# Deformable-convolution kernel: bilinear weights turned by DMA transposes, next images' preparation placed by a table over three images

## What is computed

```python
# layer 0: channel attention on the group-normalized image
q, k, v = split(gn(x) tokens @ w_qkv.T)           # each (192, 1024) per image
attn = softmax(einsum('bcn,bdn->bcd', q, k) * SCALE)
x = x + (w_out @ (attn @ v) + b_out)
# layer 1: modulated deformable 3x3 convolution on the group-normalized result
offset = clip(conv3x3(gn(x), off_w) + off_b, -8, 8)     # 18 channels: y and x of 9 taps
mask = 2 * sigmoid(conv3x3(gn(x), mask_w) + mask_b)     # 9 channels
y = sum over 9 taps of w[tap] @ bilinear_sample(gn(x), pixel + tap + offset) * mask, + proj_b
# batch norm over all 32 images, then exact GELU
x = x + gelu(batchnorm(y) * gamma + beta)
```

## Time and profile before

| | us |
|---|---|
| three runs, median (lowest to highest) | 4007.24 (3994.69 to 4007.55) |
| profiled execution, its own time | 3993.97 |
| its span | 3992.2 |

### The profile page before, as it was taken

The page is one execution under the profiler, slowest core; times in us unless marked ns, Lnnn a source line. Parts: engine busy times, 40 slices in busy tenths (PEclk is TensorE's granted clock), DMA queues, the critical chain, the costliest instruction groups (busy, mean ns, idle before and its releaser), DMA issues.

```text
span 3992.2 us, 110012 instructions
## 1 busy us (share of the span) xinstructions
PE 3544.1 (89%) x38338; PEld 3034.8 (76%) x38338; DVE 2646.4 (66%) x5834; ACT 2111.3 (53%) x4790; POOL 1412.8 (35%) x1165
## 2 busy tenths in 40 slices
PE   3999999999999999999999999999999999999700
PEld 2788887888888888888888888888888888888700
DVE  3577766676677667677766676677667667766522
ACT  1555555565555555555555565555555555555432
POOL 1333333343433333333333343333333333333311
PEclk8999999999999999999999999999999999999955
DMA  2000000000000010000000000000000001000299
GB/s 63 20 10 28 28 27 22 28 28 19 20 28 28 20 28 28 28 10 28 28 20 28 28 28 15 23 28 28 20 28 28 28 10 28 28 20 18 76 377 322
DMA packets 50722, 170.05 MB, mean 43 GB/s; under 512 B 9664, under 2 KB 10880, under 8 KB 50176
## 3 DMA queue, kind: packets, MB, share of 16 engines
q1 hardware_dynamic: 39584, 136.75, 11.2%
q0 software_dynamic: 7168, 25.17, 1.6%
q10 hardware_dynamic: 3424, 0.90, 0.1%
HBM read 87.29 MB, written 75.50 MB: 41 GB/s over the span
## 4 chain that ended last, share of the span: by engine, by line
PE 66%; DVE 12%; issue 9%; DMA 4%; POOL 3%; ACT 3%; DVEq 1%; SPq 1%; ACTq 0%; POOLq 0%
PE sps L666 10%; PE acc L683 6%; PE acc L685 6%; PE acc L684 6%; PE l L594 4%; PE zps L652 3%; PE zps L656 3%; PE zps L653 3%; PE zps L655 3%; PE zps L654 3%; DVE zl L1155 3%; DMA xn<-x_scratch 2%; POOL sT L1343 2%; DVE sl L1161 2%; PE l L526 2%
## 5 line engine op out<-in xcount | busy, mean ns | idle before, releaser
L1343 POOL TENSOR_TENSOR sT<-ay,bx 128x768 f32<-128x768 f32 x768 | 1149.5, 1507 | 1363.4 <-PE sps L666 1292.5
L1161 DVE TENSOR_TENSOR sl<-sps,sh 128x384 f16<-128x384 f32 x1536 | 846.0, 551 | 563.8 <-ACT sh L905 557.7
L683 PE MATMUL acc<-zh,sh 128*128 128x192 f16 x4608 | 1133.7, 246 | 0.9 <-issue 0.6
L685 PE MATMUL acc<-zh,sl 128*128 128x192 f16 x4608 | 1133.6, 246 | 0.0
L684 PE MATMUL acc<-zl,sh 128*128 128x192 f16 x4608 | 1133.6, 246 | 0.0
L905 ACT CAST sh<-sps 128x384 f16<-128x384 f32 x1536 | 741.7, 483 | 695.3 <-PE sps L666 689.6
L871 ACT CAST zh<-zps 128x288 f16<-128x288 f32 x1536 | 620.4, 404 | 638.8 <-PE zps L656 611.7
L1155 DVE TENSOR_TENSOR zl<-zps,zh 128x288 f16<-128x288 f32 x1536 | 693.2, 451 | 334.3 <-ACT zh L871 325.4
L666 PE MATMUL sps<-eye,sT 128*128 128x128 f32 x4608 | 785.8, 279 | 127.2 <-DVE sl L1161 99.4
L666 PEld LDWEIGHTS sps<-eye,sT 128*128 128x128 f32 x4608 | 530.9, 140 | 283.5 <-DVE sl L1161 167.9
L684 PEld LDWEIGHTS acc<-zl,sh 128*128 128x128 f16 x4608 | 450.9, 98 | 17.7 <-issue 0.8
(11 more groups left out here) (200 smaller groups left out, 6482.7 us busy)
## 6 DMA issues: line engine op xcount, KB each, us to landing
xin<-in_x SPq DMA_DIRECT2D x32, 512.0 KB, 5.4
xin<-in_x SPq DMA_DIRECT2D x64, 256.0 KB, 6.0
x_scratch<-x SPq DMA_DIRECT2D x32, 512.0 KB, 2.7
y_scratch<-ych SPq DMA_DIRECT2D x32, 512.0 KB, 2.7
zh<-y_scratch SPq DMA_DIRECT2D x20, 512.0 KB, 11.1
zl<-x_scratch SPq DMA_DIRECT2D x20, 512.0 KB, 12.5
out<-zh POOLq DMA_DIRECT2D x20, 512.0 KB, 8.6
x_scratch<-x SPq DMA_DIRECT2D x32, 256.0 KB, 3.4
```

The costliest lines, as they stand in the source:

```text
L683: pe.matmul(acc[:, 0:C], s_h, zh[:, j, ky, z], start=start and kx == 0, stop=False)
L685: mm = pe.matmul(acc[:, 0:C], s_l, zh[:, j, ky, z], start=False, stop=stop and kx == 2)
L1161: dve.tensor_tensor(one(sl), sps[u % 2][:, 0:3 * P], one(sh), ALU.subtract).then_inc(s_lo, 1)
L1343: pool.tensor_tensor(sT[:, p % ST_RING].rearrange("p k (r x) -> p k r x", r=R), a, x_, ALU.mult)\
```

## The change

1. **S is turned by DMA.** POOL writes float32 S to `s32`; ScalarE makes the high part and VectorE the low part straight from SBUF, next to each other in `spm` (128 x 2 x 768, float16), and one DMA transpose on SyncE's queue per step (`turn_s`, L499) turns the twelve 128 x 128 blocks into `sT`. TensorE's transposes and the banks `sps` are gone. A step is two units (`STEPS` = 24 an image). Rings: 2 of `s32`, 3 of `spm`, 4 of `sT`; a step's transpose is issued three steps ahead, and waits for the matmuls of the step four before it.
2. **Z in whole steps.** The two freed banks go to `zps`, so that one copy and one subtraction take 576 columns in place of 288; five steps ahead in place of ten halves.
3. **Places by table.** `part0` takes its units from `PE_AT`, `ACT_AT`, `DVE_AT`, `POOL_AT`, `SP_AT`, from -17 to 71, and `prepare` runs it for three images at once: the end of this one's preparation, the next one's, the start of the one after. The residues are cut in two halves (L1096); the second half of the hats is made during the image that uses them.
4. **Smaller moves.** Scaling y (`scale_y`) goes from VectorE to ScalarE; the stores and loads on SyncE are placed between the transposes; `rmat` shares `t1`'s memory; the far path uses other scratch.

```diff
+STEPS = 3 * TILES
+LEAD, TAIL = 17, 24
+PE_AT = {
+    "group": (-10, 21), "turn_x": (3, 3, 4, 5), "gram": 7, "t1": 9, "logits": 9, "r": 12, "m": 13,
+    "apply": (15, 16, 17, 18), "offsets": (35, 35, 35, 36, 36, 37, 37, 37), "offset_max": 11,
+}
...
+DVE_AT = {
+    "loaded": (-17, -16, -16, -14), "moments": (-12, 20), "variance": (-10, 20),
+    "residue": ((-4, -3, -1, -1), (24, 24, 26, 28)), "gram": 6, "max": 9, "softmax": 10, "m": 13,
...
-        ST_RING = 3
-        sT = sb("sT", [P, ST_RING, 3, R * W])
-        S_RING = 3
-        sh = sb("sh", [P, S_RING, 3, P], F16)
-        sl = sb("sl", [P, S_RING, 3, P], F16)
+        S_RING, H_RING = 2, 3
+        s32 = sb("s32", [P, S_RING, 3 * R * W])
+        spm = sb("spm", [P, H_RING, 2, 3 * R * W], F16)
+        T_RING = 4
+        sT = sb("sT", [P, T_RING, 12, P], F16)
...
+        def prepare(part0, u, b, par, more):
+
+            if u < TAIL:
+                part0(u + UNITS, b, par)
+            if more:
+                part0(u, b + 1, 1 - par)
+            if more == 2 and u >= UNITS - LEAD:
+                part0(u - UNITS, b + 2, par)
...
+            def turn_s(p, b):
+                sp.wait_ge(s_lo, STEPS * b + p + 1)
+                sp.sem_inc(lo_seen, 1)
+                if p >= T_RING or not first(b):
+                    sp.wait_ge(sz_done, STEPS * b + p - T_RING + 1)
+                    sp.sem_inc(slot_free, 1)
+                sp.dma_start_transpose(sT[:, p % T_RING], spm[:, p % H_RING].rearrange("p i n -> p (i n)"))\
+                  .then_inc(turned(b, p)[0], 16)
...
-            def turn_s(u, b):
-                t, ky, c = u // 6, u % 6 // 2, u % 2
+            def convolve(p, c, b, par):
+                i, ky = p // 3, p % 3
                 if c == 0:
-                    pe.wait_ge(st_made, 24 * b + 3 * t + ky + 1)
-                if u >= 2 or not first(b):
-                    pe.wait_ge(s_lo, UNITS * b + u - 1)
-                g = (3 * t + ky) % ST_RING
-                for kx in range(3):
-                    mm = pe.transpose(sps[u % 2][:, kx * P:(kx + 1) * P], sT[:, g, kx, c * P:(c + 1) * P], eye32[:, :])
-                mm.then_inc(s_ps, 1)
...
+                    pe.wait_ge(*turned(b, p))
...
+            def split_s(p, b):
+                act.wait_ge(st_made, STEPS * b + p + 1)
+                if p >= H_RING or not first(b):
+                    act.wait_ge(*turned(b, p - H_RING))
+                act.copy(spm[:, p % H_RING, 0], s32[:, p % S_RING]).then_inc(s_hi, 1)
...
+            def split_s(p, b):
+                dve.wait_ge(s_hi, STEPS * b + p + 1)
+                dve.tensor_tensor(spm[:, p % H_RING, 1], s32[:, p % S_RING], spm[:, p % H_RING, 0], ALU.subtract)\
+                   .then_inc(s_lo, 1)
...
+            def make_s(p, b, par):
...
+                if p >= S_RING or not first(b):
+                    pool.wait_ge(s_lo, STEPS * b + p - S_RING + 1)
```

More of the change, by code:

```diff
@@ L184, in build @@
         yt = bank("yt")
-        zps = bank("zps", (P, 2, 512))
-        sps = [bank(f"sps{i}") for i in range(2)]
+        zps = bank("zps", (P, 4, 512))
         l0 = [bank(f"l0_{i}") for i in range(2)]
@@ L1093, in part0 @@
-                if u == 27:
+                for q in range(4):
+                    if u == at["x1"][q]:
+                        m, n = q // 2, slice(q % 2 * 512, q % 2 * 512 + 512)
+                        dve.wait_ge(mx_ps, 4 * b + q + 1)
+                        if q == 0 and not first(b):
+                            dve.wait_ge(x1_stored, 32 * b)
+                        dve.scalar_tensor_tensor(out=x1[:, m, n], in0=l0[(q + 1) % 2][:, :], scalar=bo[:, m:m + 1],
+                                                 in1=xin[:, m, n], op0=ALU.add, op1=ALU.add).then_inc(x1_sb, 1)
@@ L1111, in part0 @@
+                for k in range(3):
+                    if u == at["move"][k]:
+                        if k == 0 and not first(b):
+                            dve.wait_ge(off_ps, b)
+                        dve.wait_ge(xn_lo, 4 * b + 2 + k)
+                        moved = move(k, b, par)
+                        if k == 2:
+                            moved.then_inc(x2_moved, 1)
+                if u == at["offsets"]:
                     dve.wait_ge(off_ps, b + 1)
@@ L1257, in part1 @@
                         flag = is_far(dve, b, par)
[L1258 to L1266 removed]
+                    for q in range(4):
+                        if u == DVE_AT["y_stats"][q]:
+                            if q < 2:
+                                y_stats(q, b, par)
+                            elif not first(b):
+                                y_stats(q, b - 1, 1 - par)
+                    prepare(part0, u, b, par, more)
                 where_far(flag, dve, b, par, more, far_pass, (fz_lo, FAR_Z), (f_st, 3 * TILES), (fs_lo, FAR_UNITS),
@@ new lines, in part1 @@
+            def part1(b, par, more):
+                lead = S_AHEAD + 1
+                if first(b):
+                    for p in range(lead):
+                        make_s(p, b, par)
+                for p in range(STEPS):
+                    if p + lead < STEPS:
+                        make_s(p + lead, b, par)
+                    elif more:
+                        make_s(p + lead - STEPS, b + 1, 1 - par)
+                    for u in (2 * p, 2 * p + 1):
+                        prepare(part0, u, b, par, more)
```

544 lines of the change are left out of this document (278 added, 266 removed).

## The result

| | median us | lowest to highest | ratio to before |
|---|---|---|---|
| before | 4002.57 | 3994.69 to 4007.55, 4 runs | |
| after | 3865.98 | 3857.68 to 3880.1, 4 runs | 0.9664 [0.963, 0.9699] |

The change saves 137 us of 4003. The forecast was 3438 us, in a range of 3290 to 3790: the direction came out, the size did not, and the time lies outside the range.

A forecast was written before the change was run, and what follows sets the result against it. TensorE, busy 89% of the span, bounds the kernel: period 115.5 - 15.8 (transposes) - 2.0 (stalls) = 97.7 us; head 97.3, 31 periods and last part 299.1 give 3425.1, as a median 3438 us, range 3290 to 3790.

The forecast's parts named there:

- Three transposes leave each of 48 units: On TensorE, removing the transposes of S saves 0.33 us a unit, 15.8 us an image.
- The prices of the pieces: Costs of the larger instructions on VectorE and ScalarE, giving 70.7 and 62.4 us an image, both under TensorE's 97.7.
- rival (a): VectorE and POOL get in each other's way: subtractions of S wait up to 1332 ns; 3625 us, chance 0.17.
- 1.8 and, for issue, up to 3 us: On SyncE's queue, the cost of one step's DMA transpose, against 4.07 us available a step.
- (b): The queue of transposes sets the pace at 4.07 to 4.8 us a step; 3760 us, chance 0.12.
- (c): Transposes go one at a time, 5.4 us each, and TensorE's clock could fall; 4430 us, chance 0.10.
- (d): Transposes cut into small pieces or blocks one by one, 14.6 us a step; 11,260 us, chance 0.02.
- the stall term: TensorE's idle time before L666, 4.0 us an image: between all and none comes back, half taken, 2.0 us.
- lands some 5 us late, within the 12.2: On SyncE, the transpose behind layer 0's stores and x loads is late but covered by the three-step lead; no cost.
- SyncE's waits: Waits for x1 and y hold up queued transposes, but are placed after VectorE's step, so costed at nothing.
- (e): The table wins back all 4.0 us of stalls and 3.5 us of other waits; 3267 us, chance 0.05.
- (f): Spreading the work does nothing for the stalls: period 99.7 us, 3501 us; shares chance 0.54 with the forecast.

The follow-up runs named there:

- e7_half: The changed kernel with a second transpose a step, of the six low blocks into a spare tile, ahead of each real one; 4048.16 us, ratio 1.0117.
- e12_third: The kernel before with one of three TensorE transposes of S a unit kept from the second image on; 3809.76 us, ratio 0.9519.
- e1_spread: The changed kernel with SyncE's plain DMAs placed one to a unit between the transposes; 3796.6 us, ratio 0.9487.
- e2_moments: The changed kernel with VectorE's moments one unit earlier, ahead of its wait for the offset convolution; 3746.17 us, ratio 0.9338.
- e11_idle: The changed kernel with plain DMAs spread, moments earlier, residues spread, offset-dependent work moved later and ScalarE's share moved into its idle time; 3657.01 us, ratio 0.9152.
- e6_bunched: The changed kernel with the next image's work bunched as in the kernel before, three units earlier; 4095.15 us, ratio 1.0226.
- e4_oneblock: The changed kernel with only one of a step's twelve blocks transposed, the others left zeros; 3759.52 us, ratio 0.94.

## Why the prediction was wrong

**Right.** "Three transposes leave each of 48 units: 48 x 0.33 = 15.8 us": 15.7 for the transposes themselves, 14.5 for all of TensorE's own work. The prices of the pieces: VectorE's subtraction of S 958 ns, measured 1006; Z's 750, measured 753; ScalarE's copy of S 0.93, measured 0.833, and of Z 0.64, measured 0.639. POOL 1567 ns for 1507. With them rival (a) falls: the two alternate as supposed (1474.0 of POOL's 1615.3 us of idle time before L1418 end with a subtraction), and a subtraction costs 48 ns more than was worked out and not 1332. The step's transpose "1.8 and, for issue, up to 3 us": the queue's share rose to 58.1% of 16 x 3878.3 us from 11.2% of 16 x 3992.2, that is 36,053 - 7,154 = 28,899 us of engine time, by 768 and 16 engines 2.35 us, a third over the 1.8; 1.42 us to issue; landing in

```profile
sT<-spm SPq DMA_TRANSPOSE x768, 3.7
```

us, under the 5 of the forecast. Rivals (b), (c) and (d) fall by this and by e7_half. DMA share went to 0.59, a little over the "fifth to a half".

On the two readings of the Trainium skill that the forecast set side by side: twelve blocks in one DMA do not take twelve times the 1309 ns of the Trainium skill ("VectorE: DVE Perf Modes", The three transpose paths), they land in 3.7 us. The 261 GB/s of the Trainium skill ("DMA: Bandwidth & Descriptors", Latency and other measured facts) would have given 1.5 us of transfer; here 393 KB took 2.35 us of the engines, 167 GB/s. Neither changed the outcome.

**Wrong, first: the stall term.** "The bounds are 4.0 us back and none ... I take half, 2.0." The bound was on the wrong side of the sign. The stalls grew from 7.5 to 14.3 us an image. The forecast read stalls before one line, L666, and took their sum as all there was to win or lose; the other engines' waits for TensorE (1292.5 us of POOL's, 689.6 of ScalarE's before S alone) were taken as slack. They are slack only while TensorE stays slow: e12_third speeds up TensorE alone, and 6.0 us come of 10.5. Applied to the changed kernel's 15.7 us, 35 to 43% would be an estimated 5 to 7 us an image that no term carried.

**Wrong, second: "lands some 5 us late, within the 12.2", by which SyncE's five DMAs were costed at nothing.** The lateness was about right: 2.4 us in the queue and 2.8 more in flight, 5.2. The 12.2 us were not there to take it. The chain in them (POOL 1.5, ScalarE 0.8, VectorE 1.0, landing 3.7) takes 7.0 even if no piece waits; the text had named these pieces but had not subtracted them before it said "within". And the pieces do wait in their queues: at unit 30 the low part was ready 5.6 us before its use, 5.6 - 3.7 = 1.9 us were left, and 5.2 - 1.9 = 3.3 of the measured 3.5 us follow. The five issues keep the queue from 1526.06 to 1531.20 us. e1_spread prices it at 69 us.

**Wrong, third: what stands in a queue behind a wait.** The forecast costed SyncE's waits one by one, but not VectorE's. The wait for the offset convolution at unit 36 with the moments behind it is worth 120 us (e2_moments), and it could be read from the table and from the order of VectorE's instructions, with TensorE's places beside them. After it, ScalarE's load from unit 41 to the image's end is likely next (e11_idle).

**Left out: the clock.** It stood only in rival (c). It is read in four windows of the changed kernel, behind the stalls of units 30 and 39:

```profile
1537.00:1541.00 4.00, 3.19 (x21) 2.87 (x22) 3.03 (x4) 0.83 (x1) 2.54 (x2) 0.65 1.11 210
1541.00:1545.00 4.00, 4.00 (x39) 3.41 (x37) 2.62 (x9) 1.37 (x2) 0.20 (x1) 0.92 0.52 97
1560.00:1564.00 4.00, 3.90 (x19) 3.64 (x20) 2.43 (x7) 1.84 (x5) 0.86 (x3) 0.50 0.18 35
1564.00:1568.00 4.00, 4.00 (x35) 3.32 (x33) 1.37 (x6) 2.04 (x4) 0.27 (x2) 0.81 0.37 67
```

After the idle 3.4 us at unit 39 TensorE works at 0.50, the 1.2 GHz level, through the next 4 us, though it is busy in 3.90 of them. The rest column rose by 3.8 us an image. How much of it is clock and how much small waits the runs do not part.

**The account.** Span forecast 3425.1, measured 3878.3, missing 453.2 us: 31 x (111.3 - 97.7) = 422, the last part 30, the head 1. Of the 13.6 us a period, 8.8 are the stalls (6.8 more, not 2.0 fewer), 3.8 the rest, and 1.3 TensorE's own work, not the transposes but the small products; these three come from images 4 to 27 and add to 13.9. By the prediction's own test, "TensorE's main wait is not for its own queue" and "the period is over 105", it had failed. "The table does better than half" had a rival for it (e) and "the spreading does nothing" another (f), but none for the case that came: spreading is worth 229 us against the bunched order of e6_bunched and still does not bring the stalls back to what they were.

## What to carry to other kernels

When the full engine gets faster, take its saving as an upper end and look for what runs a unit late behind it: here 6.0 of 10.5 us came through with nothing else changed. For each instruction that waits on the fast engine, list what stands behind it in its queue and who needs that soon; one place in a table was worth 3% of the time. Against a lead, first subtract the chain as it stands in the queues (here 5.6 us of 12.2 were left behind VectorE's part, and 3.7 of them are flight), and only then the lateness; and put a long series of plain DMAs nowhere in a row ahead of one that is waited for.

## What the runs showed that was not expected

- The clock: TensorE runs at 0.50 for some 4 us behind a stall of 3.4 us and at 0.81 for the next 4, which costs some 2.8 us again (an estimate, 4 x 0.50 + 4 x 0.19, as if all of TensorE's work there went by the clock). In the kernel before, whose longest wait within the image loop is 1.17 us, the clock stays at 1.00.
- VectorE's small SBUF instructions are lengthened too: the 128x2 products at 1557.80 and 1558.68 took 0.81 and 1.36 us, where the medians of both lines are 0.16. POOL ran two instructions over them, and each of the two products ended within 0.02 us of one of these (at 1558.59 and 1560.03). Of three copies of the same shape in the units in which the image is moved, one takes four times as long as the others, in every image but the first; it starts 0.17 us after a product of POOL (1539.61 to 1541.20 us) and ends 0.3 us behind it. The subtraction of S, which alternates with POOL, is hardly touched:

```profile
L1106 DVE COPY x2s_lo_a<-x_lo_a 128x992 f16<-128x992 f16 x32 | 53.7, 1678 | 0.0
L1106 DVE COPY x2s_hilo_b<-x_hilo_b 128x992 f16<-128x992 f16 x32 | 14.1, 440 | 0.0
```

- DMA transposes scale with their blocks: twelve cost 2.35 us of the sixteen engines. In e7_half the extra six blocks a step took (78.6% x 4042.5 - 58.1% x 3878.3) / 768 = 1.20 us, half of it, and the one block of e4_oneblock (15.8% x 3751.5 - 11.2% x 3992.2) / 768 = 0.19, a twelfth. In flight they do not: 3.7 us for twelve blocks, 2.8 for six, 2.2 for one.
- The final stage, equal in all kernels, took from 219.5 to 245.7 us in their profiles, 26 us between single profiles that says nothing of the change.
